# Graph attention on one core: a new order of work in the edge passes, and scores as two 64-row float32 products

## The reference

```
xl = x @ Wl.T + bl ; xr = x @ Wr.T + br ; e = edge_attr @ We.T
m = xl[src] + xr[dst] + e
score = where(m > 0, m, 0.2 * m) @ att
es = exp(score - segment_max(score, dst)[dst])
out = segment_sum(es / segment_sum(es, dst)[dst] * xl[src], dst) + bo
```

## Time and profile before

| | |
|---|---|
| median of 3 runs | 7471.15 us (7457.06 to 7473.19) |
| span of the profiled execution | 7464.2 us |
| TensorE busy | 5871.2 us (79%) |
| VectorE busy | 4175.9 us (56%) |
| GpSimd busy | 3043.6 us (41%) |
| ScalarE busy | 2649.9 us (36%) |
| granted TensorE clock, first pass | 0.91 of full |

### The profile page before, as it was taken

The page is one execution under the profiler, slowest core; times in us unless marked ns, Lnnn a source line. Parts: engine busy times, 40 slices in busy tenths (PEclk is TensorE's granted clock), DMA queues, the critical chain, the costliest instruction groups (busy, mean ns, idle before and its releaser), DMA issues. The chain is left out here.

```text
span 7464.2 us, 173944 instructions
## 1 busy us (share of the span) xinstructions
PE 5871.2 (79%) x40704; PEld 4054.3 (54%) x40705; DVE 4175.9 (56%) x13350; ACT 2649.9 (36%) x5416; POOL 3043.6 (41%) x3185
## 2 busy tenths in 40 slices
PE   2877778777777875677777787778788679999699
PEld 1555555555555554455555555555556663333689
DVE  6555555555555556455555555555555347888432
ACT  1333333333333332333333333333333118888210
POOL 2455555555555552555555555555553000000000
PEclk8889999999999887889998988998989889999899
DMA  3233333333333322333333333333332733332579
GB/s 82 71 80 75 80 82 82 75 82 80 74 81 83 82 73 54 75 83 79 75 81 80 75 82 82 82 76 80 82 73 59 281 141 110 115 121 94 205 287 361
DMA packets 701430, 768.13 MB, mean 103 GB/s; under 512 B 372274, under 2 KB 623257, under 8 KB 676256
## 3 DMA queue, kind: packets, MB, share of 16 engines
q1 hardware_dynamic: 553907, 574.53, 25.2%
q0 software_dynamic: 101376, 104.01, 7.3%
q10 hardware_dynamic: 46062, 88.56, 3.3%
HBM read 674.60 MB, written 88.81 MB: 102 GB/s over the span
## 5 line engine op out<-in xcount | busy, mean ns | idle before, releaser
L823 POOL DMA_INDIRECT gat_rows<-rows_scr,gat_idx x3168 | 3031.0, 957 | 2686.3 <-issue 916.2
L1049 PE MATMUL gat_counts<-adj_hot_key,adj_hot_lo 128*128 128x392 bf16 x2416 | 808.8, 359 | 930.1 <-DVE adj_hot_key L880 443.0
L973 ACT ACTIVATE gat_weights<-gat_masked,gat_newtop 128x512 f32<-128x512 f32 x792 | 571.5, 722 | 1466.4 <-DVE gat_newtop L933 1167.2
L1049 PEld LDWEIGHTS gat_counts<-adj_hot_key,adj_hot_lo 128*128 128x128 bf16 x2416 | 241.3, 100 | 1560.5 <-issue 1309.0
L987 ACT ACTIVATE gat_weightsT<-gat_tps 128x512 f32<-128x512 f32 x792 | 472.7, 597 | 1478.8 <-issue 655.8
L1094 PE MATMUL gat_sps<-gat_relu,gat_att 128*128 128x256 f32 x3168 | 970.0, 431 | 6.0 <-issue 2.7
L925 DVE COPY gat_oldtop<-gat_top 128x1 f32 x792 | 121.1, 153 | 1512.8 <-issue 860.5
L880 DVE TENSOR_SCALAR adj_hot_key<-adj_iota_key,adj_winbase,adj_key 128x392 bf16<-128x392 int16 x2416 | 950.0, 393 | 3.5 <-issue 3.3
L1114 PE MATMUL gat_aps<-gat_rows,gat_weightsT 128*128 128x65 f32 x6288 | 883.2, 288 | 16.2 <-issue 15.8
L1114 PEld LDWEIGHTS gat_aps<-gat_rows,gat_weightsT 128*128 128x128 f32 x6288 | 863.9, 213 | 9.6 <-issue 9.4
L879 DVE TENSOR_SCALAR adj_hot_lo<-adj_iota_lo,adj_low 128x128 bf16<-128x128 int16 x2416 | 677.8, 281 | 285.8 <-issue 232.3
(11 more groups left out here) (355 smaller groups left out, 7143.5 us busy)
## 6 DMA issues: line engine op xcount, KB each, us to landing
gcn_sum_adj<-adj_scr SPq DMA_DIRECT2D x98, 1568.0 KB, 8.5
gat_dstb<-dst_scr SPq DMA_DIRECT2D x792, 128.0 KB
gat_ea<-in_ea SPq DMA_DIRECT2D x792, 128.0 KB
gin_sum_adj<-adj_scr SPq DMA_DIRECT2D x49, 1568.0 KB, 8.5
adj_scr<-adj_tiles ACTq DMA_DIRECT2D x48, 1568.0 KB
at_adj<-adj_scr SPq DMA_DIRECT2D x84, 896.0 KB
gat_rows<-rows_scr,gat_idx POOLq DMA_INDIRECT x3168
gat_xr<-xr_scr SPq DMA_DIRECT2D x1584, 24.0 KB
```

The lines of the kernel that those rows point to most:

```text
L823: pool.indirect_dma_start(rows[:, u, c, 0:ROW], None, rows_d, bass.IndirectOffsetOnAxis(ap=idx[:, u, c:c + 1], axis=0)).then_inc(s_g[u], 16)
L973: act.activation(wts[:, j, :], masked[:, j, :], ACT.Exp, bias=newtop[:, j:j + 1], scale=-1.0)
L1049: return pe.matmul(bank[:, 0:WD * NT], plan.hot_lo[:, slot, :], plan.hot_key[:, slot, :], start=start, stop=False)
```

## The change

It gives all engines a new order in a visit, and it halves the rows of the score products.

- TensorE, visit k: messages of k, counts of k, turning of k-1, scores of k, sum of k-1.
- VectorE: `top` of k-2, maximum of k-1, `hit` and `miss` of k, the register loads of the counts, `oldtop` of k-1, `acc` of k-3, reduction of k-1, one-hots of k.
- ScalarE: 0.2 m of k, copy of turned weights of k-1, counts of k, then `shrink` and weights of k. A drain goes.
- The scores: for each half h a product over the 64 rows of that half alone. `sps` is one tile of two banks, a bank for each half h, and an even and an odd visit have the two halves of a bank. The reduction reads 256 columns from each bank.
- SyncE's and GpSimd's code is unchanged. A few counts at the start and the end follow the new delays.

```diff
-DRAIN = 4
+DRAIN = 3
...
-    delay = {"masked": 0, "message": 0, "fifth": 0, "relu": 1, "score": 1, "top": 2, "weight": 2, "turned": 2, "evac": 2,
-             "sum": 3, "acc": 4, "topped": 3, "olded": 2}
+    delay = {"masked": 0, "message": 0, "fifth": 0, "relu": 1, "score": 0, "top": 1, "weight": 0, "turned": 1, "evac": 1,
+             "sum": 1, "acc": 3, "topped": 2, "olded": 1}
...
-        sps = [k.ps(f"{tag}_sps{j}", [P, 512], F32, own) for j in range(2)]
+        sps = k.ps(f"{tag}_sps", [P, 2, 512], F32, own)
...
-                    dve.wait_ge(s["top"], count("top", step, 3))
+                    dve.wait_ge(s["top"], count("top", step, 2))
+                    dve.nop(nofuse=True)
+                    dve.tensor_copy(top[:, bass.ds(tb, 1)], newtop[:, (u - 2) % 2:(u - 2) % 2 + 1]).then_inc(s["topped"], 1)
+
+                    dve.wait_ge(s["fifth"], count("fifth", step, 1))
+                    j, o = (u - 1) % 2, (u - 1) % 4
+                    dve.tensor_tensor(relu[:, j, :], mps[j][:, 0:GE // 2], relu[:, j, :], ALU.max).then_inc(s["relu"], 1)
+
                     dve.wait_ge(s_loaded, step + 1)
-                    dve.nop(nofuse=True)
-                    dve.tensor_copy(top[:, bass.ds(tb, 1)], newtop[:, (u - 3) % 2:(u - 3) % 2 + 1]).then_inc(s["topped"], 1)
                     dve.tensor_scalar(hit[:, u % 4, :], near, node, None, ALU.is_equal)
...
-                    dve.wait_ge(s["sum"], count("sum", step, 4))
...
+                    dve.wait_ge(s["sum"], count("sum", step, 3))
...
+                    dve.wait_ge(s["olded"], count("olded", step, 1))
+                    dve.wait_ge(s["score"], count("score", step, 1))
+                    dve.nop(nofuse=True)
+                    dve.tensor_tensor_reduce(masked[:, j, :].rearrange("p (h e) -> p h e", h=2),
+                                             sps[:, :, j * (GE // 2):(j + 1) * (GE // 2)],
+                                             miss[:, o, :].rearrange("p (h e) -> p h e", h=2), 1.0, oldtop[:, o:o + 1],
+                                             ALU.add, ALU.min, accum_out=newtop[:, j:j + 1]).then_inc(s["top"], 1)
...
+            def weigh(step, u):
+                j, o = u % 2, u % 4
+                act.wait_ge(s["top"], count("top", step, 0))
+                act.wait_ge(s["acc"], count("acc", step, 4))
+                act.activation(shrink[:, o:o + 1], oldtop[:, o:o + 1], ACT.Exp, bias=newtop[:, j:j + 1], scale=-1.0)
                 act.wait_ge(s["turned"], count("turned", step, 2))
-                act.wait_ge(s["sum"], count("sum", step, 4))
-                act.activation(wtsT[:, j, :], tps[:], ACT.Copy).then_inc(s["evac"], 1)
+                act.activation(wts[:, j, :], masked[:, j, :], ACT.Exp, bias=newtop[:, j:j + 1], scale=-1.0
+                               ).then_inc(s["weight"], 1)
...
-                    visit(step, u)
+                    slope(step, u)
                     empty(step, u, slot, u)
+                    weigh(step, u)
...
-                    j = (u - 1) % 2
-                    pe.wait_ge(s["relu"], count("relu", step, 1))
-                    pe.wait_ge(s["top"], count("top", step, 3))
-                    for h in range(2):
-                        last = pe.matmul(sps[j][:, h * (GE // 2):(h + 1) * (GE // 2)], att[:, h, :], relu[:, j, :],
-                                         start=True, stop=True)
-                    last.then_inc(s["score"], 1)
                     if woven:
                         count_edges(step, counts[u % 2])
 
-                    j = (u - 2) % 2
-                    pe.wait_ge(s["weight"], count("weight", step, 2))
-                    pe.wait_ge(s["evac"], count("evac", step, 3))
+                    j = (u - 1) % 2
+                    pe.wait_ge(s["weight"], count("weight", step, 1))
+                    pe.wait_ge(s["evac"], count("evac", step, 2))
                     for c in range(GC):
                         last = pe.transpose(tps[:, c * P:(c + 1) * P], wts[:, j, c * P:(c + 1) * P], ident[:])
                     last.then_inc(s["turned"], 1)
...
+                    pe.wait_ge(s["relu"], count("relu", step, 0))
+                    pe.wait_ge(s["top"], count("top", step, 2))
+                    for h in range(2):
+                        last = pe.matmul(sps[:, h, j * (GE // 2):(j + 1) * (GE // 2)], att[64 * h:64 * h + 64, h, :],
+                                         relu[64 * h:64 * h + 64, j, :], start=True, stop=True)
+                    last.then_inc(s["score"], 1)
+
+                    j = (u - 1) % 2
...
-                    pe.wait_ge(s["evac"], count("evac", step, 3))
-                    pe.wait_ge(s["acc"], count("acc", step, 4))
+                    pe.wait_ge(s["evac"], count("evac", step, 1))
+                    pe.wait_ge(s["acc"], count("acc", step, 2))
```

More of the change, by code:

```diff
@@ L843, in _ @@
             dve.drain().then_inc(s_ones, 1)
-            dve.sem_inc(s["sum"], FREE + 3)
+            dve.sem_inc(s["sum"], FREE + 1)
             dve.sem_inc(s["message"], FREE)
@@ L915, in turn @@
                                       ).then_inc(s["masked"], 1)
-                    dve.wait_ge(s["fifth"], count("fifth", step, 1))
-                    j = (u - 1) % 2
-                    dve.tensor_tensor(relu[:, j, :], mps[j][:, 0:GE // 2], relu[:, j, :], ALU.max).then_inc(s["relu"], 1)
-                    dve.wait_ge(s["topped"], count("topped", step, 3))
-                    dve.wait_ge(s["sum"], count("sum", step, 4))
[L923 to L934, removed]
                     if woven:
@@ L938, in turn @@
                         dve.reg_load(pair, words[0:1, bass.ds(i * (TURN // 2) + u // 2 + 1, 1)])
+                    dve.wait_ge(s["topped"], count("topped", step, 2))
+                    dve.nop(nofuse=True)
+                    dve.tensor_copy(oldtop[:, o:o + 1], top[:, bass.ds(tm, 1)]).then_inc(s["olded"], 1)
+                    dve.wait_ge(s["sum"], count("sum", step, 3))
+                    a = acc[:, bass.ds(ta, 1), :].rearrange("p a f -> p (a f)")
+                    dve.scalar_tensor_tensor(a, a, shrink[:, (u - 3) % 4:(u - 3) % 4 + 1],
+                                             aps[:, 0:D + 1], ALU.mult, ALU.add).then_inc(s["acc"], 1)
+                    dve.wait_ge(s["olded"], count("olded", step, 1))
+                    dve.wait_ge(s["score"], count("score", step, 1))
+                    dve.nop(nofuse=True)
+                    dve.tensor_tensor_reduce(masked[:, j, :].rearrange("p (h e) -> p h e", h=2),
+                                             sps[:, :, j * (GE // 2):(j + 1) * (GE // 2)],
+                                             miss[:, o, :].rearrange("p (h e) -> p h e", h=2), 1.0, oldtop[:, o:o + 1],
+                                             ALU.add, ALU.min, accum_out=newtop[:, j:j + 1]).then_inc(s["top"], 1)
                     if woven:
@@ L948, in _ @@
                 turn(i + TAIL // TURN, False)
+            dve.drain()
+            for n in ("top", "acc"):
+                dve.sem_inc(s[n], 1)
         @block.scalar
@@ L967, in _, with slope @@
             act.sem_inc(s_stored, 16)
-            def visit(step, u):
-                j = (u - 2) % 2
[L971 to L977, removed]
+            def slope(step, u):
                 j = u % 2
@@ L1006, in half_tile @@
                 for u in range(RING):
-                    visit(first_step + u, u)
+                    slope(first_step + u, u)
                     empty(first_step + u, u, slot, a + u)
+                    weigh(first_step + u, u)
                 with nc.allow_non_contiguous_dma(reason="half a tile, once"):
@@ L1028, in _ @@
                 for u in range(TURN):
-                    visit(i * TURN + (TAIL + u), u)
+                    slope(i * TURN + (TAIL + u), u)
+                    weigh(i * TURN + (TAIL + u), u)
+            act.drain().then_inc(s["relu"], 1)
             act.wait_ge(s_stored, (half + 1) * 16 + 16)
@@ L1105, in visits @@
                     last.then_inc(s["turned"], 1)
-                    j = (u - 3) % 2
-                    v = slice((u - 3) % RING, (u - 3) % RING + 1) if back is None or u >= 3 else bass.ds(back + u, 1)
-                    if first and u < 3:
+                    j = u % 2
+                    pe.wait_ge(s["relu"], count("relu", step, 0))
[4 more added lines that the diff above has]
+                    last.then_inc(s["score"], 1)
+                    j = (u - 1) % 2
+                    v = slice((u - 1) % RING, (u - 1) % RING + 1) if back is None or u >= 1 else bass.ds(back + u, 1)
+                    if first and u < 1:
                         continue
-                    pe.wait_ge(s["evac"], count("evac", step, 3))
-                    pe.wait_ge(s["acc"], count("acc", step, 4))
+                    pe.wait_ge(s["evac"], count("evac", step, 1))
+                    pe.wait_ge(s["acc"], count("acc", step, 2))
                     for c in range(GC):
@@ L1122, in _ @@
```

(6 more changed lines are left out.)

13 lines of the change are left out of this document (6 added, 7 removed).

## The result

The changed kernel takes **8201 us** (8180 to 8215, 4 runs) against 7472 (7457 to 7476): ratio 1.098, 95% interval 1.0957 to 1.1002. The prediction was 7430 us, 7300 to 7700.

A forecast was written before the change was run, and what follows sets the result against it. It took a locked round of GpSimd's gathers and late-seen TensorE signals, 6.87 us a mean visit, as the bound. 7464 profiled, less 47 for fewer long visits, plus 7, gave 7424, stated as 7430 us; range 7300 to 7700.

The forecast's parts named there:

- Gain from the order in the locked round: 0: Edge passes: held `scores` replace held `sum`, counts start some 2 us behind the release as now; gain 0.
- the lock: Edge-pass round: four gathers after `sum`; TensorE signals due in the last gather or later seen late; 6.75 us plain round.
- SyncE's pace: Rival, edge passes: SyncE's loads set the pace, 7.05 us a visit, about 7610 us, or 7730; chance 0.33.
- The colder TensorE: Rival: TensorE's clock falls to 0.85, long visits double, +0.06 to +0.12 us a visit, 7520 to 7570; chance 0.12.
- The counts' wait: Sign of being right: TensorE's counts still wait near 1 us in a visit.
- the third case: Rival, edge passes: the lock breaks, a visit falls to 5.0 us, about 6005 us, or half that gain; chance 0.08.
- The scores: TensorE's split score products: between -0.5 and +0.2 us a visit, taken as 0 because TensorE has 2 us of room.
- wrong at its root: Sign against the forecast: TensorE signals seen on time while gathers run, or the round changes though its parts do not.

The follow-up runs named there:

- both readers held: Changed kernel, second kind of chip; GpSimd, VectorE's reduction and ScalarE's copy of turned weights all made to wait until the gathers have landed: 9810 us.
- `scores` alone: Changed kernel, first kind of chip; GpSimd and VectorE's reduction wait until the gathers have landed, ScalarE's copy of turned weights does not: 8171 us.
- `acc` early: Changed kernel with VectorE's update of `acc` right behind the maximum, before masks and registers: 5986 us on the second kind, 0.9978 of the kernel before.

## Why the prediction was wrong

**The step that failed** is "Gain from the order in the locked round: 0". It had the lock right, and that held `scores` would stand where the held `sum` had. It counted one held signal in a round. In the new order `turned` and `message` are held too, and both stand before the `sum` of the same visit: the copy of the turned weights feeds it, and the scores, which TensorE does first, need the messages. Sum and gathers then follow the release instead of meeting it. In the old order a whole visit lay between each of them and the first reader's product on TensorE. The term was 0 and should have been +0.97 us a visit: the rounds with neither late still take 6.75 us, those with one or both 8.0 to 9.9. By hand only `turned` was shown to cost (1858 us with both readers held, `scores` alone next to nothing). How the 729 us divide between `turned`, `message` and the colder clock stays open; no run took one of them out of the way on a chip of the first kind.

**The cases.** SyncE's pace is false: from 400 to 2700 us GpSimd's waits are ended by the sum (848.3 us in 251 waits) and only twice by `dstb` (0.6 us). Its working read the 14.88 us of the earlier trace rows as SyncE's pace under gathers; those three issues stand at the start of a pass, and inside the pass the mean issue of that line takes 0.4 us. The colder TensorE came, 0.81 and not 0.85, and with far more than the 0.06 to 0.12 us given to it: the 108 rounds with a cold sum (over 1.25 us) hold 108 x (9.33 - 6.87) = 266 of the 285 us lost from 400 to 2700 us. Whether a colder TensorE made those rounds long, or long pauses made it cold, is not shown. A low clock alone is not enough: at 0.86 and 0.83, in a round of 7.5 us that GpSimd sets, the orders are equal. Among rounds with only `turned` late, those with a cold sum take 8.61 us (40), the others 7.59 (50). The counts' wait, forecast near 1 us, fell to 73.5 / 294 = 0.25. The lock did break, at the very 5.0 us a visit and 6005 us of the third case; not by the change but by the chip, and without gathers on the first kind too. **The scores** were priced at 0 and were 0 on the second kind: 6088 with them and without. The note on what would make it wrong at its root, signals seen on time under gathers, was true of most chips.

**The 1.5% of the second kind.** Here one chain sets most visits: messages, scaling, maximum, masks, registers, `acc`, sum; `acc` early cuts it. But most visits are no longer than the old ones. The loss sits in each sixteenth visit, behind ScalarE's store, and the one after it. Means of the sixteenth, the next and the other fourteen, over 23 turns of each pass:

| | changed kernel | kernel before |
|---|---|---|
| first pass | 7.21, 5.86, 4.99 us | 4.60, 5.32, 5.10 us |
| second pass | 6.42, 5.55, 4.97 us | 4.47, 5.23, 5.06 us |

In the first pass ScalarE loads its table in that visit. The changed kernel, then the old one:

```profile
923.03 0.67 PE L1086 MATMUL gat_mps<-gat_ea,gat_we 128*128 128x256 f32 x2
...
924.70 1.28 ACT L976 ACT_TABLE_LOAD   x1 [1.25 <-PE gat_mps L1093]
...
926.41 0.42 DVE L914 TENSOR_TENSOR gat_relu<-gat_mps,gat_relu 128x256 f32<-128x256 f32 x1 [2.48 <-ACT gat_relu L976]
...
930.72 1.16 PE L1086 MATMUL gat_mps<-gat_ea,gat_we 128*128 128x256 f32 x2
```

```profile
902.94 0.67 PE L1079 MATMUL gat_mps<-gat_ea,gat_we 128*128 128x256 f32 x2 [0.54 <-DVE gat_miss L914]
...
903.81 1.28 ACT L973 ACT_TABLE_LOAD   x1 [1.23 <-DVE gat_newtop L933]
...
907.42 0.65 PE L1079 MATMUL gat_mps<-gat_ea,gat_we 128*128 128x256 f32 x2
```

That visit takes 7.69 us in place of 4.48. But in the second pass the trace has no such load (one at its start, against 24 in the first pass), and the visit is long there too:

```profile
2536.89 0.67 PE L1086 MATMUL gat_mps<-gat_ea,gat_we 128*128 128x256 f32 x2
...
2541.69 0.15 DVE L927 COPY gat_oldtop<-gat_top 128x1 f32 x1 [1.60 <-issue]
...
2543.27 1.16 PE L1086 MATMUL gat_mps<-gat_ea,gat_we 128*128 128x256 f32 x2
```

So the load can be only a part: the sixteenth visit grew by 2.61 us with it and by 1.95 without. Added up over 24.5 turns a pass, less the 14 other visits of a turn that each got 0.1 us shorter: 77 - 36 and 56 - 34, 63 us of the 76 between the two profiled executions. What holds the visit in the second pass is not shown; VectorE's 1.60 us have no wait that the profile knows. All this is read from the records; no run moved the load or the store. The Trainium skill (ScalarE: Activation LUTs, What ACT_TABLE_LOAD costs) gives about 1283 ns for one load; the trace agrees, 26.9 us for 21. The loads were always there: the old order had a visit of slack for them.

## What to carry to other kernels

Shortening a software pipeline takes away the slack that hides late signals and rare long visits: list, for every wait between engines, how many visits lie between signal and reader before and after, and ask what the latest arrival costs where it is now zero. A mean wait does not show this: ScalarE waited 1.8 us for the turned weights before and 2.0 after, and only what stood behind it had changed. Sort the rounds by which signal was late. And profile on more than one chip before a change of some per cent is kept or dropped.

## What the hardware showed

The same program takes 6000 us on some chips and 7388 to 7472 on others. On a chip of the latter kind, signals of TensorE that fall due near the start of the last of four indirect gathers of GpSimd are often seen late. In the kernel before, of 210 sums due within 1 us behind that start, 187 reached VectorE over 1 us late, at a median of 2.3 us behind the start; of 78 due 1.5 us or more behind it, none. Not every signal is held: of 91 turnings of the changed kernel due within 0.5 us of that start, 38 were late. GpSimd's next gather starts 3.0 us behind. On the former chips none of the 335 sums is late, with gathers of the same 1.25 us. SyncE's issues at the start of the second pass, under gathers, differ too: the earlier trace rows has three of line L783 in 14.88 us, the second kind eight in 7.11:

```profile
2280.27 7.11 SPq L783 DMA_DIRECT2D gat_xr<-xr_scr  x8
```

What differs in the chips no run shows.
